# First attention of a two-layer transformer kernel: probabilities as stationary operand, rounded products in place of transposes, scores of two heads in two row tiles

## The reference

```
x = layernorm(x)
qm, km, vm = split_heads(x @ Wq.T + bq), split_heads(ctx @ Wk.T + bk), split_heads(ctx @ Wv.T + bv)
scores = where(mask, qm @ km.T / sqrt(8), -1e8)          # 512 x 154 per head
out = softmax(scores) @ vm                                # 512 x 8 per head
x = x + concat_heads(out) @ Wo.T + bo
```

## Time and profile before

| | us |
|---|---|
| Median of 3 runs | 597.49 (597.3 to 597.72) |
| The profiled execution's own time | 596.67 |
| Its span in the trace | 594.9 |

### The profile page before, as it was taken

The page is one execution under the profiler, slowest core; times in us unless marked ns, Lnnn a source line. Parts: engine busy times, 40 slices in busy tenths (PEclk is TensorE's granted clock), DMA queues, the critical chain, the costliest instruction groups (busy, mean ns, idle before and its releaser), DMA issues.

```text
span 594.9 us, 8098 instructions
## 1 busy us (share of the span) xinstructions
PE 569.7 (96%) x2512; PEld 374.7 (63%) x2512; DVE 401.7 (68%) x1265; ACT 322.5 (54%) x566; POOL 105.4 (18%) x120
## 2 busy tenths in 40 slices
PE   4899999999999999999999899999899999999997
PEld 3556666665566667656676466666666676666664
DVE  6888989774132344666637585777889999768564
ACT  1587688766454476644855348745292542342321
POOL 3111110000111311242202432126201110100000
PEclk9999999999999999999999999999899999999999
DMA  4400000300311100101111011061321233341431
GB/s 119 195 15 10 18 10 2 105 39 19 107 36 35 54 20 19 36 28 54 60 31 44 14 42 44 1 199 39 122 75 51 90 119 98 111 138 62 143 120 56
DMA packets 23306, 38.35 MB, mean 64 GB/s; under 512 B 3776, under 2 KB 9536, under 8 KB 22880
## 3 DMA queue, kind: packets, MB, share of 16 engines
q1 hardware_dynamic: 22832, 37.44, 19.9%
q10 hardware_dynamic: 432, 0.40, 0.2%
HBM read 36.45 MB, written 1.38 MB: 64 GB/s over the span
## 4 chain that ended last, share of the span: by engine, by line
PE 80%; DVE 10%; ACT 4%; issue 2%; POOL 2%; DMA 1%; DVEq 0%; POOLq 0%; ACTq 0%
PE ps L1681 16%; PE ps L1493 9%; PE ps L1495 9%; PE ps L1851 9%; PE ps L1494 9%; PE ps L1488 3%; PE ps L1568 3%; PE ps L1588 3%; PE ps L1500 3%; PE ps L1603 2%; PE ps L1600 2%; PE ps L1758 1%; PE ps L1738 1%; DVE NM L1156 1%; PE ps L1530 1%
## 5 line engine op out<-in xcount | busy, mean ns | idle before, releaser
L1493 PE MATMUL ps<-xThi,w1s 128*128 128x512 f32 x256 | 147.5, 576 | 2.9 <-DVE h L1445 2.6
L911 ACT ACTIVATE h<-ps,early 128x512 f32<-128x512 f32 x128 | 86.7, 687 | 88.8 <-PE ps L1495 68.9
L1681 PE MATMUL ps<-h,w2s 128*128 128x512 f32 x256 | 122.5, 594 | 3.3 <-DVE ty L1245 3.2
L1495 PE MATMUL ps<-xTlo,w1s 128*128 128x512 f32 x256 | 101.4, 396 | 0.0
L1494 PE MATMUL ps<-xThi,w1s 128*128 128x512 f32 x256 | 100.9, 394 | 0.0
L1002 ACT ACTIVATE s<-ps 128x512 f32<-128x512 f32 x68 | 40.7, 598 | 95.4 <-PE ps L1495 93.8
L1493 PEld LDWEIGHTS ps<-xThi,w1s 128*128 128x128 f32 x256 | 48.5, 190 | 37.3 <-issue 18.2
L1681 PEld LDWEIGHTS ps<-h,w2s 128*128 128x128 f32 x256 | 46.2, 189 | 35.5 <-issue 23.8
L1494 PEld LDWEIGHTS ps<-xThi,w1s 128*128 128x128 f32 x256 | 48.7, 190 | 28.6 <-issue 24.3
L776 POOL TENSOR_TENSOR acc_o<-acc_o,ty 128x512 f32<-128x512 f32 x32 | 41.9, 1310 | 140.2 <-DVE ty L1245 115.7
L1445 DVE TENSOR_TENSOR h<-s,ps 128x512 f32<-128x512 f32 x68 | 46.5, 684 | 28.2 <-PE ps L1495 21.0
(11 more groups left out here) (264 smaller groups left out, 889.6 us busy)
## 6 DMA issues: line engine op xcount, KB each, us to landing
CB<-ct_rows SPq DMA_DIRECT2D x128, 128.0 KB, 2.9
WB<-wt_rows SPq DMA_DIRECT2D x32, 256.0 KB, 3.2
w2s<-w_dram SPq DMA_DIRECT2D x2, 2048.0 KB, 8.5
raw<-gu_dram SPq DMA_DIRECT2D x4, 512.0 KB, 3.8
x_in<-x_dram SPq DMA_DIRECT2D x4, 256.0 KB, 2.9
w2s<-dn_dram SPq DMA_DIRECT2D x1, 1024.0 KB, 5.7
out_dram<-ty SPq DMA_DIRECT2D x4, 256.0 KB, 2.9
late<-late_dram SPq DMA_DIRECT2D x1, 608.5 KB, 7.5
```

What stands on the lines that cost most here:

```text
L911: nc.scalar.activation(h32[:, c % HR, :], bank[c % 2], ACT.Gelu, bias=b1T[:, c:c + 1]).then_inc(b_gelu.sem, 1)
L1493: M(dst, w[0], xThi[:, x, :], start=start, stop=False)
L1495: return M(dst, w[0], xTlo[:, x, :], start=False, stop=stop)
L1681: M(bank[2], w2s[:, c * P:(c + 1) * P], h32[:, c % HR, :], start=(c % 4 == 0), stop=(c % 4 == 3)).then_inc(b_y.sem, 1)
```

## The change

Only the first attention is edited, and all five plans are new.

1. `query_stack` and `keys`: the transposes with `ident` become products in F32R with `unit`, an F32R copy of `ident` that VectorE makes once (a new step, counted on `pads`, on which the first TensorE steps wait).
2. `scores`: the four products of single heads contract only the 32 rows of their head instead of 128. Two go out together, in different row tiles and into banks 2 and 3. The product of the tails goes to bank 2 or 3 by the group's parity.
3. `values`: for each of the four query tiles i, the probabilities are the weights (128x128, F32) and the values the moving operand: first the tails (64 columns), then each head (16 columns), accumulated in bank 4 with queries on partitions. Four steps with five F32 products each take the place of the three steps. The copy to `OZ` on ScalarE, the transposes of `OZ` and the semaphores between them are gone.
4. VB becomes 16 (`VM` without its zero columns, one memset less on GpSimd), and PR becomes 10 (the four buffers `CB`, unused so early, join the ring).

The plans' core is left out of the diff, apart from the steps of the first group of `values` and the last due times.

```diff
+VB = 2 * HD
...
 PLAN_PE = {
...
-    "values": [[2680, 2885, 3144], [3395, 3518, 3707], ... [13568, 13691, 13871]],
+    "values": [[2694, 2749, 2832, 2902], [3421, 3476, 3575, 3630], ... [12062, 12128, 12183, 12238]],
...
-    "downs": ... 57210, 57296, 57466]],
+    "downs": ... 55654, 55740, 55909]],
...
+    unit = sb("unit", [P, P], F32R)
...
-    VT = sb_a("VT", [P, NG, P])
+    VT = sb_a("VT", [P, NG, HG * VB])
...
-    OZ = sb_a("OZ", [P, S])
...
-    P32 = [h32[:, i, :] for i in range(HR)] + [ty[:, i, :] for i in range(2)]
+    P32 = [h32[:, i, :] for i in range(HR)] + [ty[:, i, :] for i in range(2)] + [CB[:, i, :] for i in range(CR)]
...
+    def score_bank(g, u):
+
+        return 2 + (u % 2 if u < HG else g % 2)
...
-            nc.gpsimd.memset(VM[:, :, :, 2 * HD:VB], 0.0).then_inc(zeros.sem, 1)
-            yield
...
-                nc.scalar.activation(P32[turn % PR], bank[2 + n % 2], ACT.Exp,
+                nc.scalar.activation(P32[turn % PR], bank[score_bank(g, u)], ACT.Exp,
                                      scale=float(1 / np.sqrt(HD))).then_inc(a_exp.sem, 1)
-            yield
-            act.wait_ge(a_pv.sem, a_pv.at(b, g + 1))
-            copy(OZ[:], bank[4]).then_inc(a_oz.sem, 1)
...
+            yield
+            V.tensor_copy(unit[:], ident).then_inc(pads.sem, 1)
...
         def normalise(b, g):
-            src = four(bank[4])
+            src = bank[4][:, 0:NT * HG * VB].rearrange("p (i h d) -> p i h d", i=NT, d=VB)
             yield
-            dve.wait_ge(a_ozt_ps.sem, a_ozt_ps.at(b, g + 1))
-
-            V.reciprocal(rz[:], src[:, :, HD::VB]).then_inc(a_on.sem, 1)
+            dve.wait_ge(a_pv.sem, a_pv.at(b, g + 1))
+            V.reciprocal(rz[:], src[:, :, :, HD]).then_inc(a_on.sem, 1)
...
         def query_stack(dst, qn, g):
             for i in range(NT):
-                src = qn[:, i, HG * g:HG * g + HG, :].rearrange("p h c -> p (h c)").bitcast(F32)
-                last = nc.tensor.transpose(dst[:, i * P:(i + 1) * P], src, ident)
+                src = qn[:, i, HG * g:HG * g + HG, :].rearrange("p h c -> p (h c)")
+                last = M(dst[:, i * P:(i + 1) * P], src, unit[:], start=True, stop=True)
...
-                    nc.tensor.transpose(dst[:, gg, 0:P], src[:, 0, :], ident)
-                    last = nc.tensor.transpose(dst[:, gg, P:KW], src[0:TP, 1, :], ident[0:TP, 0:TP])
+                    M(dst[:, gg, 0:P], src[:, 0, :], unit[:], start=True, stop=True)
+                    last = M(dst[:, gg, P:KW], src[0:TP, 1, :], unit[0:TP, 0:TP], start=True, stop=True)
...
-            for u in range(NU):
-                yield
-                n = g * NU + u
-                k = 2 + n % 2
+            for u in range(0, HG, 2):
+                yield
                 if u == 0:
                     pe.wait_ge(a_q2s.sem, a_q2s.at(b, g + 1))
-                if u == HG:
-                    pe.wait_ge(a_kst.sem, a_kst.at(b, g // 2 + 1))
-                claim(k)
-                lhs = KS[:, g, u, 0:P] if u < HG else KST[:, g, :]
-                M(bank[k], lhs, QS[:, g, :], start=True, stop=True).then_inc(a_s_ps.sem, 1)
-                read_by(k, a_exp, a_exp.at(b, n + 1))
+                for j in (u, u + 1):
+                    claim(score_bank(g, j))
+                for j in (u, u + 1):
+                    q = slice(TP * j, TP * j + TP)
+                    M(bank[score_bank(g, j)], KS[q, g, j, 0:P], QS[q, g, :], start=True, stop=True).then_inc(a_s_ps.sem, 1)
+                    read_by(score_bank(g, j), a_exp, a_exp.at(b, g * NU + j + 1))
+            yield
+            pe.wait_ge(a_kst.sem, a_kst.at(b, g // 2 + 1))
+            claim(score_bank(g, HG))
+            M(bank[score_bank(g, HG)], KST[:, g, :], QS[:, g, :], start=True, stop=True).then_inc(a_s_ps.sem, 1)
...
-            pe.wait_ge(a_exp.sem, turn + HG)
-            for j in range(HG):
-                M(bank[4][VB * j:VB * j + VB, :], VM[:, g, j, :], P32[(turn + j) % PR], start=True, stop=False)
-            yield
-            pe.wait_ge(a_exp.sem, turn + NU)
-            M(bank[4], VT[:, g, :], P32[(turn + HG) % PR], start=False, stop=True).then_inc(a_pv.sem, 1)
-            read_by(4, a_oz, a_oz.at(b, g + 1))
-            yield
-            claim(4)
-            transpose4(bank[4], OZ[:].rearrange("p (i t) -> p i t", i=NT)).then_inc(a_ozt_ps.sem, 1)
+            for i in range(NT):
+                if i:
+                    yield
+                else:
+                    pe.wait_ge(a_exp.sem, turn + NU)
+                t, o = slice(i * P, (i + 1) * P), i * HG * VB
+
+                M(bank[4][:, o:o + HG * VB], P32[(turn + HG) % PR][:, t], VT[:, g, :], start=True, stop=False)
+                for j in range(HG):
+                    last = M(bank[4][:, o + j * VB:o + (j + 1) * VB], P32[(turn + j) % PR][:, t], VM[:, g, j, :],
+                             start=False, stop=(j == HG - 1))
+            last.then_inc(a_pv.sem, 1)
```

More of the change, by code:

```diff
@@ L122 @@
+    "spread_second": [[37053, 37453, 38126, 38138, 38150, 38851, 39108, 39277, 39761, 39964, 40181, 40494, 40726,
[4 rows of a table added]
 }
 PLAN_POOL = {
[L124 to L131, removed]
@@ new lines @@
+    "values": [[1918], [4844], [7456], [9965]],
+    "key_tails": [[1784, 1860], [4884, 4946], [7079, 7298], [10005, 10066]],
+    "norm_b": [[6856, 6975], [11678, 11706], [17427, 17455], [20268, 20295]],
+    "stage_b": [[13251, 14101, 14710, 15264, 15886, 16508, 17301, 17786], [19116, 19652, 20562, 23079, 23214, 23350,
+        23867, 24395], [26819, 26955, 28251, 28482, 29404, 30621, 30834, 31304], [33671, 33807, 35371, 35507, 36072,
+        37504, 38114, 38457]],
+    "split1": [[33933, 37630, 37870, 39208, 40259]],
@@ L168 @@
[L168 to L173, removed]
@@ new lines @@
+    "key_stacks": [[1466, 1501, 1535, 1570, 1608, 1741, 1776, 1811], [3392, 3487, 3522, 3758, 4528, 4563, 4598, 4633],
+        [6105, 6245, 6280, 6315, 7144, 7179, 7214, 7249], [8617, 8709, 8854, 8889, 9648, 9683, 9718, 9753]],
+    "group": [[2274, 2360, 2409, 2501, 2550, 2612], [2882, 2983, 3033, 3125, 3223, 3337], [3438, 3561, 3613, 3709,
[5 rows of a table added]
+    "output": [[4987], [7711], [10247], [12534]],
+    "prepare_b": [[10093, 11092, 12051], [13226, 14000, 17355], [20397, 22046, 24426], [27443, 28545, 30507]],
@@ L188 @@
-    "values": [[1285, 1626, 1664, 1672, 1767, 1911], [4828, 4874, 5251, 5259, 5287, 5340], [7907, 7952, 8376, 8543,
-        8551, 8705], [10786, 11220, 11257, 11396, 11404, 11412]],
-    "queries": [[1419, 1491, 1553, 1566], [3164, 3345, 3575, 3588], [6253, 6415, 7129, 7238], [9194, 9625, 9687, 9739]
-        ],
-    "biased": [[720], [2632], [3485], [6714]],
-    "split0": [[4393, 5060, 5120, 5180, 6053, 9119, 9485, 10904]],
-    "maxima": [[1834, 1873, 1927, 1965, 2026, 2064, 2119, 2158, 2208, 2227], [2248, 2319, 2427, 2466, 2555, 2594, 2692,
[9 rows of a table removed]
@@ new lines @@
+    "masks": [[870, 1067], [2487, 2826], [4667, 4836], [7435, 7592]],
+    "keys": [[1118, 1163, 1196, 1227, 1274], [1967, 2845, 2878, 2909, 2955], [5100, 5423, 5502, 5708, 5820], [7683,
+        7801, 8008, 8312, 8423]],
+    "values": [[1307, 1352, 1389, 1397, 1874, 1882], [4340, 4963, 5069, 5077, 5084, 5092], [7132, 7407, 7468, 7576,
+        7584, 7675], [9728, 9773, 10132, 10178, 10323, 10331]],
+    "queries": [[1419, 1491, 1553, 1566], [3107, 3378, 3479, 3492], [5572, 6020, 6336, 6349], [8176, 8720, 8821, 8834]
+        ],
@@ new lines @@
+    "biased": [[720], [2660], [4010], [6633]],
+    "split0": [[4146, 4608, 4674, 5350, 6200, 8116, 9149, 9798]],
+    "maxima": [[1797, 1836, 1890, 1929, 2000, 2038, 2093, 2131, 2182, 2201], [2221, 2266, 2314, 2359, 2449, 2493, 2583,
[9 rows of a table added]
+    "normalise": [[2988, 3010], [3737, 3785], [4450, 4472], [4844, 4867], [5929, 5952], [6409, 6498], [6962, 7018],
+        [7456, 7556], [8533, 8620], [8996, 9130], [9567, 9589], [9965, 10071], [10952, 10977], [11394, 11417], [11882,
+        11904], [12313, 12427]],
@@ new lines @@
+    "feed": [[22747, 22819, 22909, 23301, 23320, 23339, 23363, 23439, 23490, 23554, 23625, 24512, 24590, 24854, 24926,
[6 rows of a table added]
+    "norm_d": [[29023, 29113, 30205, 30478, 32756, 33018, 33654, 33943], [34992, 35083, 36855, 36873, 37061, 37793,
+        37812, 38314], [41578, 42165, 43116, 43267, 43286, 43913, 43931, 43982], [47911, 48001, 48530, 48549, 48567,
+        48992, 49011, 49062]],
+    "halves_d": [[34382, 36111], [40485, 41248], [44485, 46182], [49554, 49651]],
+    "router": [[35112, 35144, 35175, 35217, 35442, 35469, 35501, 35552, 35621, 35658, 35690, 35722, 35747, 35767],
[3 rows of a table added]
@@ L258 @@
+    "stage_d": [[38492, 38657, 38780, 38844, 39036, 39117, 39205, 39495, 39689, 39821, 39892, 40037, 40109, 40250,
[8 rows of a table added]
 }
 PLAN_PE = {
-    "context_keys": [[720], [1948], [5240], [8257]],
-    "context_values": [[1150], [4648], [7748], [10485]],
```

(47 more changed lines are left out.)

158 lines of the change are left out of this document (71 added, 87 removed), and 178 rows, old and new, of tables (PLAN_ACT, PLAN_DVE, PLAN_PE, PLAN_SP).

## The result

The changed kernel takes 724.41 us (median of 4 runs, 722.2 to 728.26), against 597.39 for the kernel before in the same comparison: a ratio of 1.2134 (95% interval 1.21 to 1.2167), 127 us slower. The forecast was 619.5, in a range of 602 to 638. The direction was right and the size wrong by a factor of almost six. The kernels whose clock falls differ from execution to execution by up to 4%, so a span in a trace and a median of theirs may stand some us apart; a ratio leaves out executions more than 1.5% above the fastest, and the traces of e1, e3 and e15 are of such a one.

What follows compares the result with a forecast made beforehand. TensorE's list was taken to bound the kernel: values +31, scores +2 and rounded products 0 make 33 us, less 11 absorbed by waits, +22; forecast 619.5 us, range 602 to 638.

Steps and rivals of the forecast that it cites:

- rival D: New values steps: the array streams little for 4.45 us a group, so the clock falls (sign: 0.50); chance 0.08.
- the router's burst at 125 us: Evidence cited against a falling clock: this burst of router products pulled nothing down.
- The sum: TensorE's list grows by 31 + 2 + 0 = 33 us, waits absorb 11: +22, forecast 619.5 us.
- The price of the values: Values steps: 0.111 us a record, 4.45 us a group against 2.51 before, +31.0 us on TensorE.
- Rival A: Values: a short product costs one load, 0.55 us for five products; 582 us in all; chance 0.07.
- The cover: First attention: TensorE's waits, up to 26 us, absorb 11 us: 9.7 behind the maxima plus 1 elsewhere.
- The row tiles: Scores: a pair takes 0.46 to 0.57 us against 0.46 for two single products; +2 us for 32 pairs.
- C's first half: Scores: the paired tiles don't overlap; this or exposed F32R loads add +9 to +10 us, giving 629 to 630.
- the keys' visits: Keys going in and out of a 32-row tile: 0.23 us a visit, taken as the nearer form for score pairs.
- the column tiles' price: Visit to the column tiles in the old values steps: 0.34 us, the other price for the tiled mode.
- The rounded products: Query and key transposes as F32R products: same pace, 0.111 us each, no change; bounds -9 to +10 us.
- Elsewhere: Outside TensorE's edited steps: ScalarE's 9.6 us of dropped OZ copies worth nothing by itself; unedited stages behind unchanged.

Runs made afterwards that it cites:

- e1: Kernel before with only the new values steps (probabilities as weights, ring of ten); old transposes, single scores and plan kept: 700.81 us, ratio 1.1696.
- e3: Changed kernel with each head's values zero-padded, so its products stream 64 columns instead of 16: 668.02 us, ratio 1.1069.
- e15: Changed kernel with one useless F32 product of 256 columns added ahead of each values piece: 751.41 us, ratio 1.2516.
- e4: Changed kernel with values zero-padded so that every values product, tails too, streams 128 columns: 632.1 us, ratio 1.0581.
- e8: Kernel before with the transposes of OZ written three times over, +14 us on TensorE's list: 608.8 us, ratio 1.0198.
- e11: Changed kernel with 128 moving columns in the values products and single score products instead of row tiles: 625.3 us, ratio 1.0455.
- e6: Kernel before with only the scores of two heads put in two row tiles: 611.87 us, ratio 1.0233.
- e16: Changed kernel with single score products over all 128 rows instead of row tiles, 16 moving columns kept: 685.98 us, ratio 1.148.
- e5: Kernel before with only the query and key transposes replaced by F32R products with the unit matrix: 597.55 us, ratio 1.0014.
- e2: Changed kernel and its plan with the values steps of the kernel before put back: 613.88 us, ratio 1.0275.
- e12: Changed kernel with probabilities and values rounded to F32R and 64 moving columns in each values product: 660.79 us, ratio 1.102.

## Why the prediction was right or wrong

**The step that failed: the clock, rival D.** I named it and gave it 0.08. It took nearly the whole stage, all but 17 of 256.5 us (mean clock 0.53), and decided the result. The chance rested on one piece of evidence, the router's burst at 125 us, under one microsecond of short products between long ones. That burst says nothing on a stage in which such products are about half of TensorE's time. The sum had the warning in it: 4.45 us of short products a group out of some 9. With the clock held by wider products (e4) the same loads end at 632.1, inside my range. So of the 127 us, 92 are the clock's, and 35 remain, up to 6 of them the clock's too (the start of the stage). I also overlooked a stretch at half pace in the kernel before: the earlier trace rows calls the one at 421 us the only one and the earlier trace rows has a clock of 1.00, but up to 22 us the pace is half.

**The price of the values was right.** 0.111 us a record, 1.11 a piece: measured 0.111 and 1.11 in e4, 1.02 to 1.07 in the change at full clock, where the tails' first load seems to hide in part. Rival A, 0.55 us a piece, is refuted: no piece comes near it.

**The cover was mis-sized.** I let the waits take 11 of 33 us, the 9.7 behind the maxima in the first place. In e8, with the old order, they took 2 of 14, and those 9.7 us stayed. The engines' lists are in order. My reading is this: when TensorE gets later, the maxima are made later, VectorE reads them later and TensorE waits again; such a wait moves with the work and isn't room. In the changed kernel the same wait came down to 4.6 us, so a new order can shorten it where added work alone doesn't. What its order covers follows from e11, which has the new order and no row tiles: 31 us more on the list gave 28, and up to 4.5 of those are its longer start at half clock. So 3 to 8 us were covered, not 11.

**The row tiles: right form, wrong size.** Pairs do stream together, so that C's first half is refuted. But a pair is 0.63 us, +0.17, where I took +0.06 and a bound of +0.11: I took the keys' visits as the nearer form, and the column tiles' price was nearer. That is +5 us instead of +2. What I had no term for is the clock: where it holds the tiles cost 7 us (e4 less e11), in the kernel before 14 (e6), in the change 38 (change less e16).

**The sum again at full clock.** Without the row tiles my sum gives 31 less 11, +20; e11 measured +28. These 8 us are the cover, 3 to 8 us too large, and the later rise of the clock at the stage's start, up to 4.5; the runs don't separate the two further. The row tiles were 7 us instead of 2: 3 for the pairs, up to 2 again for the start. 22, 8 and 5 make the +35 of e4.

**The rounded products: right.** 0.10 us against 0.11, and no difference in e5. The loads behind them last about as long as those of F32: 187 ns at the least in the change and a median of 192 in e5, against the 192 of an F32 load.

**Elsewhere.** The stages behind didn't move, as forecast. That ScalarE's ten microseconds were worth nothing isn't contradicted by any run, but no run isolates them.

**What stays open.** That the narrow products bring the clock down is shown (e1 against e2, e3, e4). What it is about them that does so isn't. e15 shows that long products between narrow ones don't make up for them at this dose; a larger dose wasn't tried. In e12, with 64 columns and one record a product, the clock of the stage (to 205.7 us) was 0.55, hardly above the change's 0.53; in e3, with 64 columns and two records a product, it was 0.72. Why row tiles lower the clock isn't shown either; that only 32 of 128 rows are at work in each is a likeness and no more.

## What to carry to other kernels

Before a wide moving operand is swapped for a narrow one, price two things: the weight loads that then show, and what every other product of the stage costs if the clock goes down (a rounded product 0.19 us instead of 0.10); a short burst elsewhere in the trace that left the clock alone is no evidence for a stage full of them. If such products can't be avoided, try to pad the moving operand with zeros as long as a record costs no more: here it was 0.111 us with 128 columns as with 8, and 128 instead of 16 gave 92 us back. And in a kernel with fixed orders don't count waits in full as cover for added work on the bounding engine: in the old order, of 14 us added, 12 arrived at the end, while of 14.6 us removed under 2 did. Last, compare the pace of known products with the clock that a view shows at the start of a trace, where its record may not have begun.

## What the runs showed of the hardware that I had not expected

- TensorE's records cover 254.38 of 256.5 us of the stage, and the granted clock was 0.53. With 128 moving columns in the same products it was 1.00 from 35 us on, with 64 it was 0.72 in the stage. The records' busy time doesn't tell the three apart: it is full in all of them (142.66 of 145.5 us with 128 columns, 199.38 of 202 with 64).
- At half clock the weight loads slow down as well: 333 ns against 192, and a record from 0.111 to 0.20 us. So a stretch that is bound by loads loses about as much (a factor of 1.8) as one bound by streaming (0.43 against 0.23 us for 512 columns).
- A pair of 32-row tiles pays about 0.20 us on entry (0.43 us in the chain of e4 against 0.23 for a single product) and 0.20 on leaving (two maxima products in 0.49 us behind it against 0.29). The trace shows that time is lost at each change, and doesn't show what it goes to.
